# Graph attention on Trainium2: where the factor 1 - c of a running sum is computed, and how it reaches the tiles

## The reference

```python
k = conv(x_src, edge_attr, edge_sh, ...k weights)      # per edge, 8 heads x 8
v = conv(x_src, edge_attr, edge_sh, ...v weights)      # per edge, 8 heads x 16
alpha = einsum('ehq,qk,ehk->eh', q[dst], Wdot, k)
amax  = segment_max(alpha, dst); ealpha = exp(alpha - amax[dst])
denom = segment_sum(ealpha, dst); attn = ealpha / denom[dst]
out   = segment_sum(attn[..., None] * v, dst)
```

## Time and profile before

| | us |
|---|---|
| three runs | 5260.24, 5251.45, 5254.87 (median 5254.87) |
| the profiled execution: its time | 5260.24 |
| its span, first to last instruction | 5258.5 |
| PE busy | 4410.0 (84% of the span) |
| DVE busy | 3875.1 (74%) |
| ACT busy | 2651.9 (50%) |
| POOL busy | 2052.8 (39%) |

### The profile page before, as it was taken

How to read it: one execution, slowest core, us unless ns; L and a number is a source line. 1 busy time by engine, 2 the same in 40 slices (tenths; PEclk the granted TensorE clock), 3 DMA queues, 4 the chain that set the end, 5 groups by cost and what they waited for, 6 DMA issues and landing times. The chain is left out here.

```text
span 5258.5 us, 67348 instructions
## 1 busy us (share of the span) xinstructions
PE 4410.0 (84%) x19382; PEld 2881.7 (55%) x19382; DVE 3875.1 (74%) x5975; ACT 2651.9 (50%) x4144; POOL 2052.8 (39%) x1942
## 2 busy tenths in 40 slices
PE   4666689999899999941899999999999999999923
PEld 4566567777777777731444544544544554554412
DVE  7999654545545455441589999999999999999965
ACT  4666555554555545321355555555555555555531
POOL 3333000000000000014776766666776776676522
PEclk9888899999999999955899999999999999999955
DMA  3333599899999989602577777777777777777751
GB/s 110 104 104 99 141 220 221 190 229 186 220 212 199 228 186 223 124 2 58 136 186 206 210 207 206 209 208 205 208 209 205 208 210 204 209 212 202 191 158 35
DMA packets 1843595, 930.66 MB, mean 177 GB/s; under 512 B 1316133, under 2 KB 1665955, under 8 KB 1843243
## 3 DMA queue, kind: packets, MB, share of 16 engines
q1 hardware_dynamic: 1438187, 587.52, 48.7%
q10 hardware_dynamic: 344208, 211.90, 13.2%
q0 software_dynamic: 60848, 127.02, 9.7%
HBM read 657.63 MB, written 268.32 MB: 176 GB/s over the span
## 5 line engine op out<-in xcount | busy, mean ns | idle before, releaser
L2073 POOL DMA_INDIRECT e_x_rows<-x_table,e_src x1616 | 1712.9, 1060 | 762.8 <-issue 442.5
L1144 PE MATMUL acc<-t_wide,scaled 128*128 128x512 f32 (+1 forms) x6370 | 1461.8, 388 | 129.5 <-DVE t_wide L1281 84.0
L1144 PEld LDWEIGHTS acc<-t_wide,scaled 128*128 128x128 f32 x6370 | 1163.2, 190 | 413.9 <-ACT t_wide L1162 146.8
L1162 ACT CAST t_wide<-t_ring 128x1176 fp32r<-128x1176 uint8 (+1 forms) x490 | 597.0, 1255 | 300.0 <-PE acc L1144 207.2
L1281 DVE CAST t_wide<-t_ring 128x1764 fp32r<-128x1764 uint8 (+1 forms) x490 | 535.4, 1125 | 220.1 <-PE acc L1144 216.8
L1647 POOL MEMSET l_eps<- 128x1 f32 x2 | 0.2, 100 | 1650.7 <-POOLq L1347 1641.9
L2411 DVE TENSOR_TENSOR_SCAN e_vsum<-e_factors,e_vsum,e_weighted 128x512 f32<-128x512 f32 x403 | 518.8, 1287 | 17.7 <-ACT e_factors L2275 3.4
L539 PE MATMUL lists_rows_ps<-lists_hot_lo,lists_hot_hi 128*128 128x196 fp8e4 x3200 | 371.1, 282 | 183.5 <-DVE lists_hot_hi L464 183.5
L1291 DVE TENSOR_TENSOR e_less<-e_x,e_part 128x512 f32<-128x512 f32 x101 | 70.0, 693 | 556.4 <-ACT e_part L1184 335.1
L2139 PE MATMUL e_b_lv<-e_x_gv,e_wlin_v 128*128 128x512 f32 x808 | 423.2, 605 | 64.7 <-DVE x_res L2374 33.5
L539 PEld LDWEIGHTS lists_rows_ps<-lists_hot_lo,lists_hot_hi 128*128 128x128 fp8e4 x3200 | 332.4, 109 | 221.5 <-DVE lists_hot_hi L464 206.4
(11 more groups left out here) (207 smaller groups left out, 6689.6 us busy)
## 6 DMA issues: line engine op xcount, KB each, us to landing
e_factors<-share_rows SPq DMA_DIRECT2D x404, 256.0 KB, 5.0
sums_table<-e_out_rows ACTq DMA_DIRECT2D x404, 256.0 KB
t_ring<-adjacency_bytes SPq DMA_DIRECT2D x245, 416.5 KB, 6.2
t_ring<-adjacency_bytes SPq DMA_DIRECT2D x245, 367.5 KB, 4.7
q_first<-hop_zeros_q ACTq DMA_DIRECT2D x101, 512.0 KB, 4.4
e_q_rows<-q_first SPq DMA_DIRECT2D x404, 128.0 KB
e_same_dst<-same_row SPq DMA_DIRECT2D x404, 128.0 KB
adjacency_bytes<-lists_staged SPq DMA_DIRECT2D x196, 196.0 KB, 2.7
```

Of the source, the lines that this page charges most:

```text
L1144: mm = nc.tensor.matmul(acc[c][:, 0:n], U[p][:, b, :], flat_t[:, lo:lo + n], start=(b == 0 and p == 0), stop=(b == NB - 1 and p == 1), ski ...
L1162: nc.scalar.copy(wide[g % WIDE][:, h0:h1, :], ring[g % BYTES][:, h0:h1, :]).then_inc(wide_act, 1)
L2073: nc.gpsimd.indirect_dma_start(x_rows[g % 3][:, j, :], None, x1_table, bass.IndirectOffsetOnAxis(ap=src[:, g * GT + j:g * GT + j + 1], axis=0)
```

## The change

The factor 1 - c is no longer made by ScalarE for each group from the loaded tile. VectorE makes it once per round from `weight`, with one tensor_scalar (c * -1 + 1) into a new tile `c_past`, directly behind `shares`. `share_rows` in HBM gets a second plane; SP stores `c_past` into it after `weight`, and each load of `factors` brings both planes. The 404 activations of `take_past` and their semaphore `a_past` are gone.

```diff
-     V_WACROSS, V_WNEXT, V_WINTO, V_WSUM, V_INVERSE, V_OWN) = range(1, 21)
-    N_V = V_OWN
+     V_WACROSS, V_WNEXT, V_WINTO, V_WSUM, V_INVERSE, V_OWN, V_PAST) = range(1, 22)
+    N_V = V_PAST
...
+        c_past = sb("c_past", [P, GE])
...
-        share_rows = nc.dram_tensor("share_rows", [ROUNDS * P, GE], F32, kind="Internal").ap()
+        share_rows = nc.dram_tensor("share_rows", [ROUNDS * P, 2, GE], F32, kind="Internal").ap()
...
             def store_shares(t):
                 n = groups_of(t) * H
+                rows = share_rows[t * P:t * P + n]
                 sp.wait_ge(v_round, t * N_V + V_OWN)
-                sp.dma_start(share_rows[t * P:t * P + n, :], weight[0:n, :]).then_inc(shares_out, 16)
+                sp.dma_start(rows[:, 0, :], weight[0:n, :]).then_inc(shares_out, 16)
+                sp.wait_ge(v_round, t * N_V + V_PAST)
+                sp.dma_start(rows[:, 1, :], c_past[0:n, :]).then_inc(shares_out, 16)
...
                 if row == 0:
-                    sp.wait_ge(shares_out, 16 * (t + 1))
+                    sp.wait_ge(shares_out, 32 * (t + 1))
...
-                sp.dma_start(factors[g % FACTORS][:, 0, :],
-                             share_rows[at:at + H, :].unsqueeze(0).to_broadcast([D // H, H, GE])
+                sp.dma_start(factors[g % FACTORS][:],
+                             share_rows[at:at + H].unsqueeze(0).to_broadcast([D // H, H, 2, GE])
                              ).then_inc(shares_in[g % FACTORS], 16)
...
-            def take_past(g):
-                act.wait_ge(shares_in[g % FACTORS], 16 * (g // FACTORS + 1))
-                nc.scalar.activation(factors[g % FACTORS][:, 1, :], factors[g % FACTORS][:, 0, :], ACT.Identity,
-                                     bias=ones[:, 0:1], scale=-1.0).then_inc(a_past, 1)
...
             def add_up(g):
                 dve.wait_ge(v_weighted, g + 1)
-                dve.wait_ge(a_past, g + 1)
...
                 nc.vector.tensor_tensor(weight[0:n, :], weight[0:n, :], local[0:n, :], ALU.mult).then_inc(v_round, 1)
+                own(t, V_OWN)
+                if t > 0:
+                    dve.wait_ge(shares_out, 32 * t)
+                nc.vector.tensor_scalar(c_past[0:n, :], weight[0:n, :], -1.0, 1.0, ALU.mult, ALU.add
+                                        ).then_inc(v_round, 1)
```

More of the change, by code:

```diff
@@ L1944, in edge_attention @@
         v_query = sem("v_query")
-        a_past = sem("a_past")
         v_weighted = sem("v_weighted")
@@ L2296, in exponentials @@
                 if t > 0:
-                    act.wait_ge(shares_out, 16 * t)
+                    act.wait_ge(shares_out, 32 * t)
                 nc.scalar.activation(weight[0:n, :], local[0:n, :], ACT.Exp).then_inc(a_round, 1)
@@ L2307, in _ @@
                     copy_x(2 * i)
-                if late(i):
-                    take_past(late(i)[0])
-                if now:
                     hide(2 * i)
@@ L2316, in _ @@
                     copy_rv(2 * i)
-                if late(i):
-                    take_past(late(i)[1])
-                if now:
                     hide(2 * i + 1)
```

## The result

The changed kernel takes 5305.36 us (median of 4 runs, 5295.34 to 5312.74) where the kernel before takes 5256.91 (4 runs, 5251.45 to 5260.24): a ratio of 1.0093, 95% interval 1.0078 to 1.0108. It is 48 us slower; 5259.0 was forecast, and the range ended at 5276. The profiled execution took 5309.66 us with a span of 5307.9, so the two traces differ by 49.4 us, as the timed runs do.

The account below looks back on a forecast made before the run. It took one chain through VectorE and TensorE, with TensorE waiting for the `value` product, as the bound. Clock +1.3 and tail +2.8 gave +4.1 us on 5254.87, hence 5259.0 us; range 5243 to 5276.

Parts of the forecast that it names:

- ScalarE's 404 activations, 0: Main part of edge attention: removing them frees an engine at 55%, worth 0; bounds 0 and -3.4 us.
- `c_past`, 0.43 us and 0.47 on the chain: VectorE, ahead of the awaited `value` product: the new instruction takes 0.43 us and adds 0.47 in each of 23 rounds.
- The clock, +1.3 us: TensorE in the main part: falls keep their own beat, so longer stalls cost one shift, +1.3 us in all.
- The rounds are again 98.99 us long: Main part: once 0.94 us of slow stretch lies in the stall, the added 0.47 us is given back.
- bound of +10.8: Main part: upper bound if the fall followed the stall, each of 23 rounds costing 0.47 us.
- Rival B: Main part: the fall follows the stall, so VectorE's 0.47 us is paid 23 times; +13.6 with tail, 5268.5 us; chance 0.16.
- Rival C: Main part: the moved stall keeps falls out of many rounds; half the rounds 5248.5 us, all 5230; chance 0.12.
- Hidden, with 3 us of cover, 0 us: Transfers in the main part: doubled `factors` loads land near 3579.0, read at 3582.1, costing 0 us.
- Rival D: Main part: halved load rate lands the first `factors` pair 0.6 us late in 23 rounds; +17.9, 5272.8 us; chance 0.09.
- The tail, +2.8: After the main part: shares and `c_past` 0.9, larger loads 3.6, ScalarE waits -1.7; bounds -3.4 and +8.2 us.
- estimate of 2.2: Tail groups without round work: at some 358 GB/s from HBM, 2.2 us per group instead of 1.9.
- burst figure: Tail: 288 GB/s moved where loads stand nearly alone, used to put 0.52 MB at 1.8 us.

Follow-up runs that it names:

- e4: Kernel before plus an unused `c_past` on VectorE directly behind the shares, once per round, neither stored nor loaded: 5280.07 us, ratio 1.0034.
- e9: Kernel before with the shares (L2513) moved behind the pair's first `value` product: 5224.32 us, ratio 0.9932.
- e5: Kernel before without ScalarE's 404 activations, the scan taking c in place of 1 - c: 5260.48 us, ratio 0.9997.
- e2: Kernel before with the doubled transfers alone: shares stored twice, both halves loaded, ScalarE still computing 1 - c: 5296.36 us, ratio 1.0067.
- e1: Changed kernel with three `out_rows` buffers instead of two, `c_past` in the tile of `lift`: 5293.50 us, ratio 1.0059.
- e6: Changed kernel with `c_past` made once per round by ScalarE and three `out_rows` buffers: 5275.15 us, ratio 1.0027.
- e12: Changed kernel with three `out_rows` buffers and `c_past` moved behind the `value` product: 5274.03 us, ratio 1.0030.
- e11b: Changed kernel, two buffers, with `c_past` moved behind the first `value` product, the repeated timing: 5314.46 us, ratio 1.0104.
- e3: Changed kernel with `c_past` made once per round by ScalarE instead of VectorE, two buffers: 5302.52 us, ratio 1.0076.
- e8: Kernel before plus an unused `c_past` at the end of VectorE's pair, behind the last `value` product: 5262.35 us, ratio 1.0000.

## Why the prediction was wrong

- **What bounds the kernel: right.** One chain through VectorE and TensorE, with the stall ahead of L2139 on it (e4, e9).
- **ScalarE's 404 activations, 0: right** (e5, -0.3 us in the pairs).
- **`c_past`, 0.43 us and 0.47 on the chain: right** (0.43 and 0.46; the stall 2.6).
- **The clock, +1.3 us: mis-sized; e4 measured +16.0.** "The rounds are again 98.99 us long" holds for 18 of 22. The step had the restart drift behind the fall until 0.94 us of overlap balance the 0.47. It does not get there: at 0.66 us and more a second slow stretch follows the first, the next restart comes after 100.8 us, where the ones just before came after 99.2, and the drift begins anew from 0.9 us ahead. The bound of +10.8 was too small too, since it took a slow stretch to be always 3.4 us. Rival B had about the size of the loss (13.6), but only half of its mechanism: the restarts are some 99.4 us apart in most rounds, while the falls never are (98.99 or 102.4), and the other half is the doubled stretches. Rival C's falls that stay out came too: four rounds of the changed kernel and 16 of e2, with their cause not found.
- **"Hidden, with 3 us of cover, 0 us", the step that failed.** What it says of the loads holds in the main part. It asked only whether the doubled loads land in time, and not what else uses the DMA engines. The sums' stores do, with two buffers and a ScalarE in order behind them; they became late, 19.3 us in the pairs by e1. A row was there to warn, though the prediction did not have it among its own: the kernel before already had this wait in its tail, 2.1 us, once. Rival D had the cause (DMA engines at 0.97) at the wrong place: it let VectorE wait for `factors`, which no row of the main part shows.
- **The tail, +2.8: mis-sized; +20.5 measured,** +19.2 by the transfers alone (e2). It counted two loads behind each store at the 288 GB/s of a 1.5 us stretch. The eight loads there are paced by the transfers, 2.3 us a group (the near hit of the estimate of 2.2 is chance: it counted 0.79 MB for a group, where 2.53 MB moved in 10 us, some 0.58 for each; and 0.79 MB in 1.92 us are 410 GB/s, not 414), and the late stores hold up ScalarE for 43.0 us; three buffers give back 6.5 (e1). The rest stays with every kernel that loads both halves, 10.7 to 15.9 (e6, e12). How it divides between the loads and what waits behind them was not separated.
- **The sum.** In the pairs 31.3 = 19.3 (stores, e1) + 13.4 (place of `c_past`, e12 against e1) - 1.4. The order matters: with two buffers the second step gives nothing (e11b). In the tail 20.5 = 6.5 + 14.0.

The burst figure was the wrong one for a sum over a run of loads: after the change the DMA engines, at a share of 1.0, moved 249 GB/s over the main part and 253 among the tail's loads. The Trainium skill (DMA: Bandwidth & Descriptors, Specifications) asks for transfers of at least 512 B for the full rate and gives some 358 GB/s as the limit of HBM for one core. The 249 and 253 GB/s lie below that figure, and the small packets do not explain it here: over the main part 248,384 of 574,341 packets are under 512 B, with 8% of the bytes, but among the tail's loads (5060 to 5070) practically all bytes are in packets of 512 B to 8 KB, and the rate is the same. What sets it, no run shows.

The late stores cost +9.1 us in the pairs of e2, +17.9 in e3 and +41.8 in e11b. The table of TensorE's time has the parts: 30 to 52 us of waits for ScalarE come in, and falls of the clock that stay out give 24, 13 and 10 back. Open is why so many falls stay out behind stalls of the same 2.1 us, and why ScalarE waits for the stores 111.2, 128.5 and 160.1 us at nearly the same transfers; no run holds one of these fixed.

## What to carry to other kernels

Before moving work from an engine to the DMA queues, list everything that already uses them, and for each its buffers and who waits in order behind it: a load can stay hidden while a store that shares its engines becomes the stall. Ahead of a stall that carries a fall of the clock, an instruction can cost more than its length: 0.43 us a round came to 16.5 us, 10.5 of them longer stalls and the rest the clock. Try moving the work behind the instruction that is waited for (+16 us became 0, and moving the shares gained 36). Test two suspected causes together as well as alone: here taking `c_past` off its place gave 7 us (e3) or nothing (e11b) until the stores had their third buffer, and with it 14.

## What the runs showed of the hardware

- A slow stretch of TensorE's clock between the pairs' first and last products was 3.4 or 6.8 us long (10.2 too on the slower chip below). After stalls of 2.1 us (before, e5, e8, e12) all were 3.4, one in each round; but in e2, with stalls of that length in all rounds but one (1.6), 16 of 23 rounds had none. After 2.6 us (e4) 18 of 23 were 3.4 and five 6.8; after 1.5 us (e9) 18 of 23 rounds had none.
- A 256 KB store of the sums, back within 10.8 us in the kernel before (DMA share 0.77 over the main part), took up to 15.3 us from issue to release after the change (1.12 during that store; 38 late ones, 11.9 in the median). A DMA share of 1.0 to 1.12 moved 249 to 257 GB/s, in the main part and among the tail's large packets alike. The store of the first half of the shares still landed after 2.0 us in the median, the second after 2.9.
- One chip ran the kernel before in 5582.62 us where the others took 5257 to 5264, with a scatter of 1%. Its cause was not looked for further.
